# Mamba-2 layer and feed-forward on one core: the place of the decay spreads on TensorE and of the second slot's convolution start on ScalarE

## The reference: what is computed

```python
proj = einsum('bsd,de->bse', rmsnorm(x), in_proj_w)      # z | xBC | dt
xBC = silu(depthwise_conv4(xBC) + conv_b)                # over tokens
xs, Bg, Cg = split(xBC)                                  # 32 heads x 64, 8 groups x 64, 8 groups x 64
dt = softplus(dt_raw + dt_bias); dA = exp(dt * -exp(A_log))
h_t = dA_t * h_{t-1} + dt_t * x_t (outer) B_t            # per head, state 64 x 64
y_t = h_t C_t + D * x_t
out = rmsnorm_per_group(y * silu(z)) * gate_norm_w @ out_proj_w
```

## Time and profile before

| what | us |
|---|---|
| median of 3 runs | 1287.64 |
| the runs | 1285.94 to 1288.23 |
| the profiled execution | 1288.33 |
| its span, first to last instruction | 1286.5 |

### The profile page before, as it was taken

One profiled execution on the slowest core, in us unless ns is written; L12 is line 12 of the kernel. 1 busy time (PEld: TensorE's weight loads), 2 busy tenths in 40 slices (PEclk: granted clock), 3 DMA queues, 4 the chain that ended last, 5 costly groups with the idle time before them and its releaser, 6 DMA issues.

```text
span 1286.5 us, 29886 instructions
## 1 busy us (share of the span) xinstructions
PE 1097.4 (85%) x8970; PEld 726.5 (56%) x8970; DVE 1121.1 (87%) x1967; ACT 973.6 (76%) x2798; POOL 887.3 (69%) x600
## 2 busy tenths in 40 slices
PE   0524788999899989998999899989999999987786
PEld 0513566666566656665666566656666666653565
DVE  8788899999789988998999889988999989857995
ACT  2556788888688878887888888878888888852453
POOL 6560367878587867786778778776878788894321
PEclk9998899999899999999999999999999999997999
DMA  5500000000000000000000000000000000100301
GB/s 150 181 0 0 10 2 2 1 2 2 28 2 2 2 28 2 2 2 28 2 2 2 28 2 2 2 27 2 2 2 10 10 2 2 34 26 27 107 25 33
DMA packets 28803, 25.44 MB, mean 20 GB/s; under 512 B 12112, under 2 KB 22992, under 8 KB 28368
## 3 DMA queue, kind: packets, MB, share of 16 engines
q1 hardware_dynamic: 24400, 21.18, 5.4%
q10 hardware_dynamic: 4224, 2.10, 0.5%
HBM read 14.88 MB, written 8.39 MB: 18 GB/s over the span
## 4 chain that ended last, share of the span: by engine, by line
PE 39%; DVE 25%; issue 16%; ACT 12%; POOL 4%; ACTq 1%; DMA 1%; DVEq 1%; POOLq 0%; SPq 0%
DVE conv L1077 8%; PE bank L1441 5%; PE bank L1458 5%; ACT xw L760 5%; DVE lm L1066 4%; PE bank L1464 4%; PE bank L1385 4%; ACT conv L768 3%; PE bank L1401 3%; PE bank L1496 3%; PE bank L1387 3%; PE bank L1386 3%; PE bank L1417 2%; PE bank L1473 2%; DVE cdec L1107 2%
## 5 line engine op out<-in xcount | busy, mean ns | idle before, releaser
L1077 DVE SCALAR_TENSOR_TENSOR conv<-bank,cw,conv 128x511 f32<-128x511 f32 (+2 forms) x576 | 410.1, 741 | 32.6 <-ACT conv L768 30.2
L1066 DVE TENSOR_TENSOR_SCAN lm<-bank,ident 128x512 f32<-128x512 f32 x256 | 298.5, 1208 | 63.8 <-PE bank L1401 51.6
L615 POOL TENSOR_TENSOR lm<-lm,cbs 128x1024 f32<-128x1024 f32 x128 | 303.3, 2369 | 57.0 <-ACT xw L760 56.4
L798 ACT ACTIVATE xdt<-bank,dt_all 128x64 f32<-128x64 f32 x1024 | 222.6, 332 | 0.0
L601 POOL TENSOR_TENSOR gated<-gated,gate 128x512 f32<-128x512 f32 x128 | 164.2, 1283 | 68.9 <-DVE gated L1116 61.1
L760 ACT ACTIVATE xw<-xdt,lm 128x64 f32<-128x64 f32 x768 | 196.3, 339 | 11.7 <-issue 11.7
L621 POOL TENSOR_TENSOR ssum<-ssum,sq 128x512 f32<-128x512 f32 x96 | 123.2, 1284 | 90.9 <-ACT sq L812 88.3
L1385 PE MATMUL bank<-xn_hi,w_hi 128*128 (+1 forms) x320 | 153.2, 479 | 27.9 <-DVE conv L1077 26.0
L607 POOL TENSOR_TENSOR gated<-gated,rbs 128x512 f32<-128x512 f32 x128 | 164.9, 1289 | 1.3 <-ACT rbs L861 1.3
L1441 PE MATMUL bank<-gated,w_out 128*128 128x512 f32 x256 | 151.9, 677 | 4.9 <-POOL gated L607 3.1
L1458 PEld LDWEIGHTS bank<-lm,xdt 128*64 128x64 f32 x2048 | 110.7, 138 | 80.2 <-issue 79.5
(11 more groups left out here) (183 smaller groups left out, 1832.9 us busy)
## 6 DMA issues: line engine op xcount, KB each, us to landing
lm<-in_L_attn_in_proj_w SPq DMA_DIRECT2D x1, 2048.0 KB, 9.8
xn_scratch<-chan SPq DMA_DIRECT2D x4, 512.0 KB, 4.8
r_stage<-residual_scratch SPq DMA_DIRECT2D x8, 256.0 KB, 3.2
x_scratch<-r_stage SPq DMA_DIRECT2D x8, 256.0 KB, 2.3
cbs<-x_scratch SPq DMA_DIRECT2D x8, 256.0 KB, 2.9
gated<-x_scratch SPq DMA_DIRECT2D x1, 2048.0 KB, 8.0
out_tokens<-gated ACTq DMA_DIRECT2D x8, 256.0 KB, 2.3
xn_stage<-xn_scratch SPq DMA_DIRECT2D x7, 256.0 KB, 2.9
```

Of the source, the lines that this page charges most:

```text
L615: gp.tensor_tensor(lm[:, mr, :, :], lm[:, mr, :, :], cbs[:, :, :], ALU.mult).then_inc(m_done, 1)
L798: act.activation(xdt[:, r, at:at + HP], misc_of("xt", n)[:, at:at + HP], ACT.Copy, scale=dt_h).then_inc(xdt_done, 1)
L1066: V.tensor_tensor_scan(lm[:, m % R, a, :], bc_bank[(3 * m + a) % 2][:, :], ident4[:, :], 0.0, ALU.mult, ALU.add).then_inc(scanned, 1)
L1077: V.scalar_tensor_tensor(out=conv[:, ci % 4, shift:S], in0=tile_bank(b, n, t)[:, 0:S - shift], scalar=cw[:, q, t, KW - 1 - shift:KW - shif ...
```

## The change

On TensorE the first two spreads of the next slot leave the end of the slot: the first (k = 0) is issued right behind y, ahead of the variance sums and the bt transposes; the second (k = 1) right behind the projection of z, ahead of cb, rbc, xn and xo. On ScalarE weighing and the first step of the convolution become two local functions; in the second slot of a unit (r = 1) the convolution is issued first, in the other slots weighing as before. No instruction is added or taken away, and no DMA is touched.

```diff
             def slot(b, n):                       # ScalarE
                 q, r = divmod(n, R)
                 real = not (isinstance(b, int) and b == NB)
-                weigh = back(b, n, LAG_M)
-                if weigh is not None:
...
-                if real:
-                    for t in PLAN[r]:
...
+                def weigh_x():
+                    weigh = back(b, n, LAG_M)
+                    if weigh is not None:
...
+                def convolve():
+                    if real:
+                        for t in PLAN[r]:
...
+                if r == 1:
+                    convolve()
+                    weigh_x()
+                else:
+                    weigh_x()
+                    convolve()
                 prev = back(b, n, 1)
@@ TensorE
                     last.then_inc(y_ready, 1)
+                ahead = back(b, n + 1, LAG_SSD)
+                if ahead is not None:
+
+                    spread(*ahead, 0)
                 if r == 0 and back(b, n, LAG_VAR) is not None:
...
                 if ssd is not None:
                     project(b, n, "z", ssd)
+                if ahead is not None:
+
+                    spread(*ahead, 1)
                 if r == 0 and ssd is not None:
...
                     last.then_inc(xo_ready, 1)
-                if back(b, n + 1, LAG_SSD) is not None:
-
-                    for k in range(2):
-                        spread(*back(b, n + 1, LAG_SSD), k)
```

More of the change, by code:

```diff
@@ L762, in slot @@
-                if real:
-                    for t in PLAN[r]:
[L765 to L769, removed]
+                def weigh_x():
+                    weigh = back(b, n, LAG_M)
+                    if weigh is not None:
+                        bb, m = weigh
+                        mr = m % R
+                        after(act, scanned, 2 * SLOTS, bb, 2 * m + 1)
+                        xdt_there(act, bb, m)
+                        after(act, s_ready, SLOTS, bb, m - 2)
+                        for c in range(CH - 1):
+                            for a in range(2):
+                                half = slice(HP * a, HP * a + HP)
+                                act.activation(xw[:, mr % 2, c, half], xdt[:, mr, P * c + HP * a:P * c + HP * a + HP], ACT.Copy,
+                                               scale=lm[:, mr, a, P * c + P - 1:P * c + P]).then_inc(xw_done, 1)
@@ new lines, in convolve @@
+                def convolve():
+                    if real:
+                        for t in PLAN[r]:
+                            ci = CONV_ORDER.index((q, t))
+                            after(act, proj_ready, NCONV, b, ci)
+                            after(act, silu_done, NCONV, b, ci - 4)
+                            act.activation(conv[:, ci % 4, :], tile_bank(b, n, t)[:, :], ACT.Identity,
+                                           scale=cw[:, q, t, KW - 1:KW], bias=cb_bias[:, q, t:t + 1]).then_inc(acc_init, 1)
```

## The result

The changed kernel takes 1328.9 us (median of 4 runs, 1326.0 to 1329.9), against 1286.8 us before in the same comparison: a ratio of 1.0326, with a 95% interval of 1.0301 to 1.0352. It is slower by 42 us; 48 were forecast. The profiled execution took 1328.1 us, with a span of 1326.3.

What follows compares the result with a forecast made beforehand. ScalarE's late block was to push the third slot, where it and VectorE are level. Terms 43 + 1 + 3 + 1 = 48 us on the profiled 1288.3 gave 1336.3, 1336 as a median; range 1306 to 1361 us.

Steps and rivals of the forecast that it cites:

- What bounds: Main stage: one loose place per unit, before the second slot's taps; ScalarE and VectorE level at the third slot.
- Part 1: TensorE, first slot: two spreads at 0.22 us each delay cb, cbs, the second slot's transposes and projection by 0.44.
- Part 2: ScalarE, second slot: convolution starts 0.11 us later, against 0.33 gained if spreads were free; block from weighing 1.54 late.
- Part 3: TensorE, second slot: with the spread ahead of rbc, rbs starts 1.38 us late, lost each unit; 31 x 1.38 = 43 us.
- ScalarE's own bound: ScalarE, second slot: its block is 1.54 us late; the 0.44 gap before the gate absorbs some, leaving at least 1.10.
- the signs that it named: Scans' wait under 15 us; taps' wait up 60 to 110; ScalarE idle 1 us a unit; rbs and unit period 1.4 later.
- What else moves: Outside the main term: fourth slot's gate 1 us, next batch's input transposes 3 us, output transposes 1 us.
- The input's transposes: TensorE, 7 times: now behind the second spread, each late by nothing to 0.44 us, taken as 3 us in all.
- POOL's cover: POOL: lm's wait for weighing that ends 3 us later is covered by gaps of 1.72 and 1.26 us, 2.98 in all.
- B: Scans set the pace: second slot's taps at most 0.33 us earlier, 10 us gained, 1278 us; chance 0.07.
- C: Second slot's taps lose 0.11 us and the third slot absorbs ScalarE's delay: 3 us, 1291 us; chance 0.08.
- D: TensorE's clock falls in each second slot's idle, stretching work by some 0.8 us, 25 us in all: 1361 us; chance 0.07.

Runs made afterwards that it cites:

- Run 6: The change with second slots' weighing issued in first slots, their projections ahead of x transposes, and the second spread last except in first slots: 1276.8 us.
- Run 1: The change's moved spreads alone, with ScalarE's old order (weighing first everywhere) kept: 1333.6 us, 1.0371 of the kernel before.
- run 2: The kernel before with only the convolution put ahead of weighing in the second slot, spreads left at the slot's end: 1308.6 us, ratio 1.0168.
- run 3: The change with the second spread put behind the rbc transposes in second slots alone: 1325.4 us, 1.0303 of the kernel before.
- runs 3 to 5: After run 3: the change with the second slot's weighing issued in the first slot, 1325.4 us; then both edits together, 1301.6 us.
- run 7: The kernel of Run 6 with the convolution ahead of weighing in third slots too: 1261.2 us, 0.9790 of the kernel before.

## Why the prediction was right

**What bounds.** Right. No instruction became slower; VectorE's wait went from the scans to the taps, and the third slot, where ScalarE and VectorE were level, is where 31.7 of 39.8 us were lost.

**Part 1** named the wait of the second slot's transposes for cbs. Run 6 shows it: with the projections ahead of them, the wait that the convolution first had brought ScalarE is gone. Its size was a little high: the two spreads moved cbs by (668.72 - 666.40) - (644.77 - 642.81) = 0.36 us, not 0.44, which is 0.18 a spread against the 0.22 of the chain. Run 1 shows the same 0.36 at the second slot's taps.

**Part 2** put the convolution at 0.11 later; it was level (+0.02), for the same reason. Its 0.33 us for spreads that cost nothing is just what run 2 measured.

**Part 3 is the term that was too large:** 1.38 us a unit and 43 us, where third slots lost 1.02 and 31.7 us. Two things made it so. The start: ScalarE's block was to be 1.54 late and is 1.42 (670.76 - 666.40 = 4.36 behind the skip, against 645.75 - 642.81 = 2.94), so xdt starts 1.45 late and ends 1.41 late, not 1.54. The chain from xdt to rbs: the prediction gave it 2.34 us, and it took 677.90 - 675.78 = 2.12. The bt transposes start 0.05 behind xdt's end and not 0.13 (a step for which no row was given), z follows them by 0.42 and not 0.60; only rbc follows z by 1.01 and not 0.92, the spread included. ScalarE's own bound was 1.10 in the prediction and is 0.84 in run 3. The prediction had both bounds in one chain, ScalarE's below and TensorE's above it; runs 3 to 5 show that both are real, 0.84 and 0.85 us with the other taken away, and 1.02 together. What it did not see is that the moved spreads would cost as much as the whole change with ScalarE's order untouched (run 1). Of the signs that it named, the scans' wait, the taps' and ScalarE's idle came as said; rbs came 1.04 us later relative to the second slot's taps (6.33 behind them, 5.29 before) and not 1.4, by this same term.

**What else moves.** Taken as 5 us; first slots alone measured 7, and second slots 1.7. That the sum of 48 comes within 8 us of the 39.8 is in part luck, as this error runs against that of Part 3. The input's transposes were bounded by 0.44 us each and cost 0.57. The bound left out that they ran, before, in the time in which the last spread waits for cdec, and now start behind that wait (the spread's weight load waited 0.47 us for cdec). Run 6, where that spread stands behind the input's transposes, shows it: they cost 0.11 us there. Three rows of the changed kernel show the wait (spread's weight load, transposes, VectorE's next step):

```profile
692.12 0.10 PEld L1410 LDWEIGHTS bank<-da_parts,sel 96*128 96x128 bf16 x1 [0.47 <-DVE cdec L1116]
...
692.35 0.60 PE L1291 MATMUL bank<-ident,xn_stage 128*128 128x128 f32 x4
...
693.96 0.69 DVE L1155 TENSOR_TENSOR xn_lo<-bank,xn_hi 128x512 f32 x1 [1.24 <-ACT xn_hi L832]
```

and two of the kernel before, where the transposes ran ahead of cdec's end and VectorE waited half as long:

```profile
667.13 0.60 PE L1282 MATMUL bank<-ident,xn_stage 128*128 128x128 f32 x4
...
668.73 0.69 DVE L1146 TENSOR_TENSOR xn_lo<-bank,xn_hi 128x512 f32 x1 [0.64 <-ACT xn_hi L823]
```

POOL's cover held: it waits 149.3 us for the weighing ahead of lm (56.4 before), and less behind it: 31.0 instead of 61.1 us for VectorE ahead of its gated product, and 73.1 instead of 88.3 us ahead of ssum. Fourth slots cost nothing (-0.6 us), where 1 was set.

**The rivals.** B (faster by 10 us) fell: the third slot has no slack that the timeline hides. C fell with it. D did not come: the idle ahead of the bt transposes was 0.51 us, not 0.9, and a projection matmul of 0.48 us follows it (676.25), as in mid-unit before. The granted clock is 1.00 from 664 to 696 us of the changed kernel: the upper level, 2.4 GHz. The Trainium skill (TensorE: Matmul & The Clock Gate, What's actually happening) says that an idle array falls back to half its clock; the trace of before agrees behind its idle of 3.11 us, where the granted clock is 0.64 from 603.5 to 607.5 us, and the changed kernel shows no fall behind 0.51 us.

## What to carry to other kernels

A long wait in front of an instruction says that it is late, not that it sets the pace: follow the chain to the next thing its engine needs, here tile 3's convolution, before paying to shorten the wait. On an engine that runs its list in order, an instruction moved forward takes its wait along and holds what stood in that gap (rbc, the input's transposes), and moving work behind a late arrival is only free where that engine has a gap to absorb it: the same exchange made in the second slot cost the next one 0.83 us (run 2), and made in the third it cost nothing (run 7). When two bounds lie this close together (0.84 and 0.85 us), taking away either shows next to nothing (3.5 us each here, 27 together), so try them together before calling a cause disproved.

## What the runs showed of the hardware that was not expected

A spread added between two fp32 products cost TensorE about 0.18 us (from y's second part to cb it is 0.36 longer with two of them: 667.53 - 664.58 = 2.95 against 643.58 - 640.99 = 2.59), less than the 0.22 of the chain and far less than its own row of 0.39. Beyond that nothing: what was moved takes as long as before (a spread of the decays 0.393 us against 0.388, a weighing 0.338 against 0.339).
